# Split rings for two broadcast rows, gates in two transfers, a new order of turns, and 39 products with zero weights in a hand-ordered kernel

## The reference, cut to what matters

```
x = x + 0.5 * ffn(norm(x))        # 128 -> 512 -> 128, GELU, ternary weights      thread F
x = x + attn(norm(x))             # a small selective scan, 16 states             thread F
x = x + 0.5 * ffn(norm(x))        # the order in the code: ffn, attn, ffn         thread F
x = x + 0.5 * moe(norm(x))        # "moef": encoder, router, 8 experts            threads P, E
x = x + mamba(norm(x))            # convolution, 256 channels x 16 states, scan   threads P, S
x = x + 0.5 * moe(norm(x))        # "moeb": the same weights again                threads P, E

# inside mamba, for every channel d and state n:
state[t] = exp(A[d,n] * delta[t,d]) * state[t-1] + delta[t,d] * u[t,d] * B[t,n]
y[t,d]   = sum over n of state[t] * C[t,n]
```

## Time and profile before

| | |
|---|---|
| time, median of 3 runs | 1186.02 us (1185.41 to 1189.14) |
| time of the profiled execution | 1187.36 us |
| its span | 1185.6 us |
| granted TensorE clock, mean over the span | 0.904 of full speed |
| busy: TensorE, VectorE, ScalarE, GpSimd | 943.9, 734.6, 674.6, 595.0 us |
| DMA: bytes moved, mean share of the 16 engines | 151.79 MB, 36.1% |

### The profile page before, as it was taken

The page is one execution under the profiler, slowest core; times in us unless marked ns, Lnnn a source line. Parts: engine busy times, 40 slices in busy tenths (PEclk is TensorE's granted clock), DMA queues, the critical chain, the costliest instruction groups (busy, mean ns, idle before and its releaser), DMA issues.

```text
span 1185.6 us, 11091 instructions
## 1 busy us (share of the span) xinstructions
PE 943.9 (80%) x3350; PEld 438.6 (37%) x3350; DVE 734.6 (62%) x1653; ACT 674.6 (57%) x1073; POOL 595.0 (50%) x476
## 2 busy tenths in 40 slices
PE   6456986798789978997899789997998679867645
PEld 4333343343344334433444443343443333422311
DVE  3213216873789559774988298738884688289711
ACT  3344575676567667657675877475775444433211
POOL 2121236552765565565656465727653666266412
PEclk9767798899899999999899999998899789988956
DMA  3002007350626064425523363425360635155220
GB/s 127 10 0 81 1 3 252 112 177 19 240 107 250 1 223 153 178 71 164 212 94 155 109 224 140 152 50 210 112 244 11 249 142 214 55 196 197 96 80 9
DMA packets 40747, 151.79 MB, mean 128 GB/s; under 512 B 2544, under 2 KB 10864, under 8 KB 38640
## 3 DMA queue, kind: packets, MB, share of 16 engines
q1 hardware_dynamic: 40688, 151.09, 36.1%
HBM read 148.20 MB, written 2.88 MB: 127 GB/s over the span
## 4 chain that ended last, share of the span: by engine, by line
PE 41%; DVE 24%; ACT 14%; DMA 8%; POOL 7%; issue 7%; SPq 0%; DVEq 0%; POOLq 0%; ACTq 0%
DVE dA L975 11%; PE yp L1482 8%; DMA bcast<-held 5%; ACT L125 4%; PE pp L1360 4%; PE mp L1440 4%; POOL dbu L706 3%; PE mp L1425 3%; PE fp L1246 3%; DVE hs L980 3%; PE pp L1226 3%; PE fp L1262 2%; PE mp L1226 2%; PE mp L1450 2%; PE pp L1330 2%
## 5 line engine op out<-in xcount | busy, mean ns | idle before, releaser
L706 POOL TENSOR_TENSOR dbu<-du,bcast 128x1024 f32<-128x1024 f32 x128 | 301.2, 2354 | 142.6 <-DMA bcast<-held 82.2
L975 DVE TENSOR_TENSOR_SCAN dA<-dA,dbu 128x512 f32<-128x512 f32 x256 | 312.7, 1221 | 82.6 <-POOL dbu L706 48.3
L1482 PE MATMUL yp<-hs,ident 128*128 128x512 f32 x512 | 282.2, 660 | 59.2 <-DVE hs L980 59.0
L1204 ACT ACTIVATE dA<-delta,pr 128x512 f32<-128x512 f32 x256 | 173.7, 685 | 119.9 <-DVE hs L980 119.2
L980 DVE TENSOR_TENSOR hs<-dA,bcast 128x512 f32<-128x512 f32 x256 | 177.0, 691 | 9.3 <-PE yp L1482 0.6
L1482 PEld LDWEIGHTS yp<-hs,ident 128*128 128x128 f32 x512 | 92.3, 205 | 188.5 <-DVE hs L980 118.9
L125 ACT ACT_TABLE_LOAD x109 | 139.8, 1283 | 18.9 <-POOL delta L629 17.0
L656 POOL TENSOR_TENSOR he<-he,gsp 128x512 f32<-128x512 f32 x64 | 81.0, 1270 | 61.3 <-ACT he L1171 37.0
L1425 PE MATMUL mp<-cont,ex_ 64*128 64x512 f32 x128 | 77.4, 686 | 20.6 <-DVE he L938 19.5
L1429 PE MATMUL mp<-cont,ex_ 64*128 64x512 f32 x128 | 77.8, 690 | 1.7 <-ACT he L1171 1.6
L1262 PE MATMUL fp<-w,hT 128*128 128x129 f32 x512 | 66.6, 280 | 12.3 <-ACT sq L1021 5.7
(11 more groups left out here) (214 smaller groups left out, 1417.1 us busy)
## 6 DMA issues: line engine op xcount, KB each, us to landing
bcast<-held SPq DMA_DIRECT2D x104, 1024.0 KB, 5.8
gsp<-gheld SPq DMA_DIRECT2D x16, 2048.0 KB, 9.6
xin<-L_attn_x SPq DMA_DIRECT2D x8, 256.0 KB, 5.2
out<-xb SPq DMA_DIRECT2D x8, 256.0 KB, 2.4
ex_<-c_ex SPq DMA_DIRECT2D x1, 985.0 KB, 7.1
bcast<-c_ps SPq DMA_DIRECT2D x1, 768.0 KB, 8.5
pr<-c_pr SPq DMA_DIRECT2D x1, 567.0 KB, 9.4
held<-dbc SPq DMA_DIRECT2D x8, 64.0 KB, 1.6
```

What stands on the lines that cost most here:

```text
L706: pool.tensor_tensor(out=dbu[:, j % 2, :].rearrange("p (r t) -> p r t", r=2), in0=d, in1=b_n, op=ALU.mult).then_inc(dbu_r.sem, 1)
L975: dve.tensor_tensor_scan(out=dA[:, half], data0=dA[:, half], data1=dbu[:, j % 2, half], initial=0.0, op0=ALU.mult, op1=ALU.add).then_inc(h ...
L1204: act.activation(out=dA[:, r * SEQ:(r + 1) * SEQ], in_=delta[:, i % 2, c, :], func=ACT.Exp, scale=mA[:, c, 2 * k + r:2 * k + r + 1]).then_ ...
L1482: pe.matmul(yp[:, :], lhsT=ident[:, :], rhs=hs[:, j % 2, r * SEQ:(r + 1) * SEQ], start=(s % PAIRS == 0 and r == 0), stop=(s % PAIRS == PAI ...
```

## The change

- **Rings.** `bcast` is split into `b_row` and `c_row`, three slots each (the same memory), with a semaphore for each slot. Each load of 1024 KB becomes two of 512 KB. A slot of B waits for the product with B alone, a slot of C for the products with C alone. SP issues B and then C of a step.
- **Gates.** The DMA of 2048 KB becomes two of 1024 KB, experts 0 to 3 and 4 to 7, each with its own semaphore; the first may go when half of the turn before is done. The products wait for their half.
- **Turns.** mpre(i+2) and the front of moef(i+3) come before the front of moeb(i), for every i; the E thread has back of f(i+3) ahead of back of b(i). All five strings are new.
- **Products with zeros.** TensorE has a fifth thread K, 39 steps, placed between the others from the first scan to the end of the last: a product of a 128 x 128 tile of zeros with 256 columns of `w1`, added to `yp` with no wait and no signal (it adds nothing). GpSimd sets the zeros once.
- **Setup.** TensorE makes the two totals of the ternary weights one after the other and only then centres `w1`; before, the centring came between them. The second total has another place in PSUM.

```diff
-P_TURNS = [... ("front" f0), ("mpre", 0), ("front" f1), ("mpre", 1), ("front" f2)]
-for _i in range(BATCH):
-    P_TURNS += [("mout", _i), ("front", M_TURNS.index(("moeb", _i)))]
-    if _i + 2 < BATCH:
-        P_TURNS.append(("mpre", _i + 2))
-    if _i + 3 < BATCH:
-        P_TURNS.append(("front", M_TURNS.index(("moef", _i + 3))))
+FRONTS = "f0 m0 f1 m1 f2 o0 m2 f3 b0 o1 m3 f4 b1 o2 m4 f5 b2 o3 m5 f6 b3 o4 m6 f7 b4 o5 m7 b5 o6 b6 o7 b7".split()
...
-SLOTS = 3
+FILL = 256
+B_SLOTS, C_SLOTS = 3, 3
...
+class Rows:
+    def __init__(self, slots):
+        self.slots, self.slot, self.load, self.after = slots, {}, {}, {}
+        free_after, loads = [-1] * slots, [0] * slots
+        for j in range(BATCH * STEPS):
+            i, s = divmod(j, STEPS)
+            twin = i * STEPS + 2 * PAIRS - 1 - s
+            if PAIRS <= s < PAIRS + slots:
+                self.slot[j], self.load[j] = self.slot[twin], self.load[twin]
+                continue
+            at = min(range(slots), key=lambda x: free_after[x])
+            loads[at] += 1
+            self.slot[j], self.load[j], self.after[j] = at, loads[at], free_after[at]
+            free_after[at] = twin if PAIRS - slots <= s < PAIRS else j
...
-                        if LOADED_AFTER[j] >= 0:
-                            sp.wait_ge(dbu_r.sem, LOADED_AFTER[j] + 1)
-                            sp.wait_ge(hc_r.sem, 2 * (LOADED_AFTER[j] + 1))
-                        src = held[i % 2, :, 2 * k:2 * k + 2, :].rearrange("(a s) r t -> a s (r t)", a=1)
-                        sp.dma_start(bcast[:, SLOT_OF[j], :, :], src.broadcast_to([P, 2, 2 * SEQ])
-                                     ).then_inc(bc_in[SLOT_OF[j]], 16)
+                            if B_ROWS.after[j] >= 0:
+                                sp.wait_ge(dbu_r.sem, B_ROWS.after[j] + 1)
+                            src = held[i % 2, 0:1, 2 * k:2 * k + 2, :].rearrange("a r t -> a (r t)")
+                            sp.dma_start(b_row[:, B_ROWS.slot[j], :], src.broadcast_to([P, 2 * SEQ])
+                                         ).then_inc(b_in[B_ROWS.slot[j]], 16)
+                        if j in C_ROWS.after:
+                            yield True
+                            if C_ROWS.after[j] >= 0:
+                                sp.wait_ge(hc_r.sem, 2 * (C_ROWS.after[j] + 1))
+                            src = held[i % 2, 1:2, 2 * k:2 * k + 2, :].rearrange("a r t -> a (r t)")
+                            sp.dma_start(c_row[:, C_ROWS.slot[j], :], src.broadcast_to([P, 2 * SEQ])
+                                         ).then_inc(c_in[C_ROWS.slot[j]], 16)
...
+                    for part in range(2):
+                        yield True
+                        some = slice(part * EP, (part + 1) * EP)
+                        if part == 0:
+                            sp.wait_ge(g_out.sem, g_out.at(m, 16))
+                        if m >= 1:
+                            sp.wait_ge(her_e.sem, her_e.at(m - 1, EP // 2 * (part + 1)))
+                            sp.wait_ge(her_o.sem, her_o.at(m - 1, EP // 2 * (part + 1)))
+                        src = gheld[m % 2, some, :].rearrange("(a e) t -> a e t", a=1)
+                        sp.dma_start(gsp[:, some, :], src.broadcast_to([P, EP, SEQ])
+                                     ).then_inc(g_in[part].sem, 16)
...
-                    if k == 0:
-                        pool.wait_ge(g_in.sem, g_in.at(m, 16))
+                    if k % 2 == 0:
+                        pool.wait_ge(g_in[k // 2].sem, g_in[k // 2].at(m, 16))
...
-                        pool.wait_ge(bc_in[SLOT_OF[j]], 16 * LOAD_NO[j])
+                        pool.wait_ge(b_in[B_ROWS.slot[j]], 16 * B_ROWS.load[j])
...
+                            if r == 0:
+                                dve.wait_ge(c_in[C_ROWS.slot[j]], 16 * C_ROWS.load[j])
...
+            def k_thread():
+                for _ in range(ORDER["PE"].count("K")):
+                    yield True
+                    pe.matmul(yp[:, 0:FILL], lhsT=zeros[:, :], rhs=w1[:, 0:FILL], start=False, stop=False,
+                              skip_group_check=True)
```

More of the change, by code:

```diff
@@ L47 @@
+M_TURNS = [({"f": "moef", "b": "moeb"}[_t[0]], int(_t[1])) for _t in FRONTS if _t[0] in "fb"]
+P_TURNS = [({"m": "mpre", "o": "mout"}[_t[0]], int(_t[1])) if _t[0] in "mo" else
+           ("front", M_TURNS.index(({"f": "moef", "b": "moeb"}[_t[0]], int(_t[1])))) for _t in FRONTS]
 ORDER = {
     "SP":
-        "AGAGBBBBBBABBGBGBBBBBBBBBBABBBGBGBBGBGBBBDBBBBBABBGBGGGBBBBBBDBBBBABBBGBGBBGBGBBBBBBBBABBGDBGGGBBBBB"
-        "BDBBBBBBBGBGBBGBGBBDBBBBBBBBGBGBGBGBBBBBBBBBBBGBGBBBBDBDGGD",
+        "AGAGGBBBBBBBBBBBBBBBBABGBGBGBBBBBBBBBBBBBBBBBBBBBBABBGGBBGBBBBBBBBBBBBBBBBBBBBABBBBBBGGGBGGGBBBBBBBB"
+        "BBBDBBBBBBBBBBABBBGGGBBBGGGBBBBBBBBBBBBBBBBBBBBBBBDBBBGGAGGGGBBBBBBBBBBDBBBBBBBBBBBBBBBGBGGBGGGBBBBB"
+        "BBBBBDBBBBBBBBBBBBBBBBBGGBGGGGBBBBBBBBBDBBBBBBBBBBBBBBBBBGGGBBBBBBBBBBGGGDDGGGD",
@@ L130, with loads_before @@
 STEPS = IC * PAIRS
[L131 removed]
+FILL = 256
+B_SLOTS, C_SLOTS = 3, 3
 STEP_ORDER = [(0, k) for k in range(PAIRS)] + [(1, k) for k in reversed(range(PAIRS))]
[L135 to L154 removed]
+class Rows:
[12 more added lines that the diff above has]
+            free_after[at] = twin if PAIRS - slots <= s < PAIRS else j
+    def loads_before(self, at, j_end):
+        return sum(self.slot[j] == at for j in self.after if j < j_end)
+B_ROWS, C_ROWS = Rows(B_SLOTS), Rows(C_SLOTS)
 PACKS = {
@@ L189, in build @@
         ones = sb("ones", [P, P])
+        zeros = sb("zeros", [P, P])
         mean32 = sb("mean32", [P, 32])
@@ L381, in build @@
         g_out = signal("g_out", 16)
-        g_in = signal("g_in", 16)
+        g_in = [signal(f"g_in{k}", 16) for k in range(2)]
         dn = Norm("d_", 2)
@@ L431, in build @@
         yg = sb("yg", [P, IC, SEQ])
-        bc_in = [sem(f"bc_in{k}") for k in range(SLOTS)]
+        b_in = [sem(f"b_in{k}") for k in range(B_SLOTS)]
+        c_in = [sem(f"c_in{k}") for k in range(C_SLOTS)]
         dA_r = signal("dA_r", STEPS)
@@ L488, in spread @@
                     if i >= 2:
-                        for s in range(SLOTS):
-                            used = sum(SLOT_OF[j] == s and j in LOADED_AFTER for j in range((i - 1) * STEPS))
-                            sp.wait_ge(bc_in[s], 16 * used)
+                        for rows, arrived in ((B_ROWS, b_in), (C_ROWS, c_in)):
+                            for at in range(rows.slots):
+                                sp.wait_ge(arrived[at], 16 * rows.loads_before(at, (i - 1) * STEPS))
                     sp.dma_start(held[i % 2, :, :, :].rearrange("s n t -> (s n) t"), dbc[64:96, :]
@@ L722, in ternary @@
                 dve.wait_ge(tot_ps.sem, k + 1)
[L723 removed]
+                step(dve.tensor_scalar(out=q[:, 0:1], in0=tot[k], scalar1=1.0 / (D * HIDDEN),
                                        scalar2=1e-5, op0=ALU.mult, op1=ALU.max))
@@ L980, in s_thread @@
                             dve.tensor_tensor(out=hs[:, j % 2, half], in0=dA[:, half],
-                                              in1=bcast[:, SLOT_OF[j], 1, half], op=ALU.mult).then_inc(hc_r.sem, 1)
+                                              in1=c_row[:, C_ROWS.slot[j], half], op=ALU.mult).then_inc(hc_r.sem, 1)
                         if s % PAIRS == PAIRS - 1:
```

121 lines of the change are left out of this document (47 added, 74 removed).

## The result

The changed kernel takes **1156.22 us** (median of 4 runs, 1156.12 to 1156.5), the one before 1185.72 beside it: a ratio of 0.9748, 95% interval 0.9727 to 0.9769. It is 29.5 us faster where 75 were forecast, outside the forecast's own 1095 to 1130, inside the range of 1078 to 1165, and nearest to rival 1 (1144).

What follows compares the result with a forecast made beforehand. TensorE, busy 80% of the span, was taken as fullest but not full, the middle periods nearly bound by it. Terms -18, -4, -31, -8, -11, -3 and 0 sum to -75 us: 1111 us, forecast 1095 to 1130, 8-in-10 range 1078 to 1165.

Steps and rivals of the forecast that it cites:

- rival 1: TensorE is the bound; work moved out of the hole lengthens the scan by as much: 1144 us (1130 to 1175), chance 0.23.
- half of its idle time in the four middle periods: New turns recover half of the 61.8 us TensorE idles in the four middle periods: 31 us.
- The holes should nearly close from scan 3 on: VectorE's pauses between scans of successive sequences: under 15 us from scan 3 on, above 25 us at the first.
- `hx(3)` was to come sooner: At the second boundary, hx(3), a scan's input, no longer queues behind a back of 34.3 us.
- the cover of one step: In the scans, split rings let B's load come one step (3.7 us) earlier, covering 0.6 us and some lateness.
- the terms of -18 and -4: Last period and last scan: three B/C loads on the chain, -18 us; two halved first loads of a scan, -4 us.
- forecast -11: Period 1, 127 us long: loses one of two backs but takes on eight letters F; gain 11 us.
- (-8): Period 0: its hole stays, so a third of TensorE's 24 us of idle time is gained, 8 us.
- -3 forecast: Gates in two transfers: in the tail the wait falls from 7.05 to 4.3 us, -3 us; elsewhere hidden.
- The fourth rival: Halved loads follow each other in one queue, periods of 124 us, last scan above 101: about 1220 us, chance 0.05.
- forecast 0: The 39 zero products on TensorE, cost against clock won: taken as nothing, ends +18 and -57 us.
- a clock of 0.9 in the last two stages: Sign that zero products work: TensorE's granted clock at 0.9 or more in the last two stages.

Runs made afterwards that it cites:

- e2: New turns and strings alone, with the old ring of joint loads, one gate transfer and no zero products: 1177.2 us, ratio 0.9934 to the kernel before.
- e6: Changed kernel with Gelu and Silu replaced by Tanh and Softplus by Exp, so one table serves all (other outputs, a probe): 1119.5 us, ratio 0.9451.
- e16: Changed kernel with each of the 39 zero products done four times, 156 in all: 1189.6 us, ratio 1.0037 to the kernel before.
- e5: Changed kernel with mout(i+1) put ahead of the front of b(i) for four sequences: 1168.3 us, ratio 0.9851 to the kernel before.
- e1: Kernel before with the split rings and split gates alone, old turns and strings, no zero products: 1170.9 us, ratio 0.987.
- e4: Changed kernel with the gates in one transfer of 2048 KB again: 1167.1 us, ratio 0.985 to the kernel before.
- e15: Kernel before with the split rings for B and C alone, one gate transfer, no zero products: 1175.3 us, ratio 0.9913.
- e3: Changed kernel without its 39 zero products: 1154.4 us, ratio 0.9736 to the kernel before.
- e12: Changed kernel with zero products only at the ends, 42 ahead of the first S and 16 behind the last: 1150.8 us, ratio 0.9707 to the kernel before.

## Why the prediction was wrong, and where it was right

**The step that failed** is "I take half of its idle time in the four middle periods: 61.8 / 2 = 31 us", together with "The holes should nearly close from scan 3 on", on which it stands. The middle periods gained 0.1 us. The pauses between sequences shrank by a third, and new ones of about the same size opened inside the scans (118 + 28 us before, 82 + 76 after); their lengths stay within two microseconds in e2 and e6. TensorE's idle time was treated as room for the work moved; it is waiting inside one order that four engines keep by their strings. That is what the delays show: on ScalarE, busy 60% of the span, 42 us added at three places in different threads cost 42 to 50 us. ScalarE, idle 40% of the span, had nothing to give at these places; and of 47 us put on TensorE itself (e16) 33 show.

**What a hole's length told** was read wrongly too: `hx(3)` was to come sooner by the `back` of 34.3 us no longer ahead of it; it came 6 us sooner in its period (80.6 to 74.3), and the preparation behind it took 11 us longer. Other turns that now stand between are the likely reason; no run takes them out one by one.

**Rival 1** (TensorE is the bound, the holes close for nothing) had the better number, 1144, and half of its mechanism: work moved out of the hole did lengthen the scan by as much, and the middle stayed at 124 us. But TensorE isn't full there (88.6% busy, and e6 takes 18.4 us off the same work), and added work shows by 0.7, not whole. It is nearer to say that the order of all strings is the bound than that one engine is; that is argued from e5, e6, e16 and the delays, for no order was found that shortens the middle.

**Rings**: the loads left the chain as the cover of one step said, and the terms of -18 and -4 were oversized. The rings alone gave 2.7 + 4.8 = 7.5 us in the two last stages: three loads of 18.1 us and two first loads on the chain were worth 7.5 us, so something else was late soon behind them. Of these 7.5 the changed kernel lost 5 again (110.2 to 112.1 and 80.9 to 84.0 us, e1 against after). Most likely it is the work that comes back there: three more letters E in the last scan, which I priced at nothing, and seven more letters P (6 to 13 in TensorE's string), which I had not seen.

**Turns**: period 1 -14.3 (forecast -11), period 0 -1.3 (-8). The reading behind the -11 was wrong: from the first S of scan 1 to that of scan 2 TensorE's string has one letter F more (22 to 23), not eight, and besides the 8 letters E it loses 7 letters P (22 to 15), the same 7 that return in the last scan. That the number came near is in part luck. The start's -6.8 was not foreseen: it is there in e2 (-7.8) and not in e1 (-0.6), which has the new setup products too, so it comes with the strings and not with the transfers or the setup. I had no term for it. Which letters give it was not tried. The tail, with five more letters E, got 3.3 us shorter in e2, its granted clock 0.74 where before has 0.62; the fuller tail may have paid for itself by the clock, which no run separates.

**Gates**: -3 forecast; 11 us under the new turns. The tail's part was sized rightly, 7.05 to 4.3 us for what is waited for (the tail's other 3.3 us come with the turns, e2); the piece in the chain of after:

```profile
1118.47 4.31 DMA gsp<-gheld
```

The rest, 5.4 us in the middle periods and 2.3 in the last scan by which e4 is longer there, I had called hidden; the chain of e4 has six loads of gates on it, that of after two. Waits for `gsp` on GpSimd and VectorE were 37.3 us before and are 23.5 after; with the new order and one gate they are 48.9.

The Trainium skill (DMA: Bandwidth & Descriptors, Measured) would have transfers of 1 MiB and more; the rings' loads are below that and did no harm here: 5.0 and 4.1 us to landing beside 5.8 for twice the size. The fourth rival, slower by the halved loads, is refuted by e15, which has them halved and is about 10 us faster.

**Zero products**: forecast 0, measured 1.8 us the other way with intervals that overlap. The number is right. The sign named for them, a clock of 0.9 in the last two stages, told nothing: it is 0.90 and 0.92 with them, 0.89 and 0.92 without (e3), and it came with the turns.

**Open** stays which order of the turns would use the 56 us that TensorE idles in the middle periods: one exchange was tried (e5) and lost 12 us. Also open is how far the strings fit the very durations they have: 138 to 161 us taken off ScalarE brought a sixth to a quarter, 42 us put on it cost all. That the strings fit the durations they now meet would explain it; no run tests it.

## What to carry to other kernels

Where every engine works through a fixed order, idle time isn't slack: put a known delay at two or three unrelated places before you forecast a gain from it; if each costs in full, moving work may only move the hole, as it did here. Add up the pauses of the engine that matters over a whole period, between the phases and inside them, not only the one the change aims at. And don't price a transfer on the chain by its length: the gain ends where the next thing is late, and a run with that part of the change alone gives it.

## What the hardware showed that I had not expected

- **Less work for TensorE, slower kernel.** With the sum thinned to 64 columns the granted clock of the middle periods fell from 0.96 to 0.83 (before: 0.96 to 0.84) and the time rose by 26.6 and 34.3 us. Products with zeros raise it: 0.76 to 0.89 in the tail by 16 of them, for 5.1 us; and 0.84 to 0.93 in the start by 42 (e12), for nothing that shows.
- **Taking table loads away brings little.** 1283 ns each, 161.7 us in all, and with 125 of them gone only 36.8 us come back. The Trainium skill (ScalarE: Activation LUTs, What ACT_TABLE_LOAD costs) gives the same 1283 ns, and 2.66 us for a switch with its drain; in the trace of after a load at 593.83 us ends at 595.11 and the next ACTIVATE starts at 595.12, so no drain shows behind it; of the 126 loads 114 are followed within 0.05 us by the next instruction of ScalarE. The measurement decides: in this kernel a load costs its 1283 ns.
- **Half the bytes, less than half the gain.** 512 KB land in 5.0 and 4.1 us where 1024 KB took 5.8; my line through two medians said 3.9. In the tail a single transfer of 2048 KB took 7.05 us, and the first half of 1024 KB, with the second issued right behind it, 4.31.
